# Parameter chains on GpSimd, rotation products summed in PSUM, second half's statistics between the first half's scalings

## What is computed

```python
u = group_norm(x)                                   # 16 x 96 x 256
fx = _layernorm(u, ln1_g, ln1_b)
step = jnp.exp(log_step)
lam_bar = jnp.exp(lam * step)                       # 48 complex modes
B_bar = ((lam_bar - 1.0) / lam)[:, None] * Bc
Bu = jnp.einsum('ph,blh->blp', B_bar, fx)
# xs[l] = lam_bar * xs[l-1] + Bu[l]
y = 2.0 * jnp.real(jnp.einsum('hp,blp->blh', Cc, xs)) + D * fx
y = jax.nn.gelu(y, approximate=False) + fx
fy = _layernorm(y, ln2_g, ln2_b)
z1, z2 = jnp.split(fy @ W_enc.T, 2, axis=-1)
out = x + (z1 * jax.nn.gelu(z2, approximate=False)) @ W_dec.T + fy
```

## Time and profile before

| | us |
|---|---|
| median of 3 runs | 112.12 (110.3 to 112.47) |
| profiled execution | 110.42 |
| its span | 108.6 |
| TensorE matmul busy | 94.9 (87%) |
| VectorE busy | 77.6 (71%) |
| ScalarE busy | 41.0 (38%) |
| GpSimd busy | 31.9 (29%) |
| granted TensorE clock, mean | 0.961 |

### The profile page before, as it was taken

The page is one execution under the profiler, slowest core; times in us unless marked ns, Lnnn a source line. Parts: engine busy times, 40 slices in busy tenths (PEclk is TensorE's granted clock), DMA queues, the critical chain, the costliest instruction groups (busy, mean ns, idle before and its releaser), DMA issues.

```text
span 108.6 us, 1488 instructions
## 1 busy us (share of the span) xinstructions
PE 94.9 (87%) x502; PEld 56.2 (52%) x502; DVE 77.6 (71%) x260; ACT 41.0 (38%) x79; POOL 31.9 (29%) x26
## 2 busy tenths in 40 slices
PE   5999897269989929999899999999599999999960
PEld 4668766146555715676476655567324432533310
DVE  1688999999986899658677302389990289994590
ACT  2254167807449100024037009818049722024200
POOL 8600000400049992000018000007995000296000
PEclk9999999955799999999999999999999999999997
DMA  2997000000000000000000000000000000450135
GB/s 77 275 262 168 3 0 0 6 0 0 0 0 0 0 0 3 0 6 0 0 0 0 0 0 3 6 0 0 0 0 0 0 0 0 118 149 29 28 84 177
DMA packets 3767, 3.79 MB, mean 35 GB/s; under 512 B 496, under 2 KB 3664, under 8 KB 3760
## 3 DMA queue, kind: packets, MB, share of 16 engines
q1 hardware_dynamic: 3392, 3.49, 12.3%
q10 hardware_dynamic: 368, 0.20, 0.8%
HBM read 2.12 MB, written 1.57 MB: 34 GB/s over the span
## 4 chain that ended last, share of the span: by engine, by line
PE 70%; DVE 21%; issue 4%; ACT 1%; DVEq 1%
PE ps L424 70%; DVE st L836 2%; DVE fy L664 2%; DVE pm L885 2%; DVE sc L694 2%; DVE rs L664 1%; DVE upper L668 1%; DVE sq L664 1%; DVE tb L664 1%; DVE tb L668 1%; DVE y L982 1%; DVE gn L664 1%; DVE rs L694 1%; DVE fx L664 1%; DVE sc L664 1%
## 5 line engine op out<-in xcount | busy, mean ns | idle before, releaser
L424 PE MATMUL ps<-fy,mt 96*96 96x512 f32 x32 | 14.9, 600 | 1.3 <-DVE fy L664 1.3
L290 POOL TENSOR_TENSOR y<-gl,fx 96x512 f32<-96x512 f32 x4 | 6.1, 1524 | 29.8 <-ACT gl L379 29.8
L298 POOL TENSOR_TENSOR res<-fy,xs 96x512 f32<-96x512 f32 x8 | 10.7, 1359 | 11.6 <-DVE fy L664 11.5
L424 PE MATMUL ps<-xs,pm 96*96 96x256 f32 x32 | 10.8, 492 | 3.3 <-DVE pm L885 3.3
L385 ACT ACTIVATE y<-ps,vecs 96x512 f32<-96x512 f32 x8 | 5.5, 687 | 16.4 <-PE ps L424 16.4
L664 DVE SCALAR_TENSOR_TENSOR w<-ps,vecs,y 96x512 f32<-96x512 f32 x8 | 5.9, 743 | 7.4 <-ACT y L385 7.4
L424 PE MATMUL ps<-fx,dm 96*96 96x512 f32 x16 | 8.4, 605 | 2.6 <-issue 2.2
L933 DVE TENSOR_TENSOR Z<-Z,ps 96x240 f32<-96x240 f32 (+3 forms) x8 | 2.8, 355 | 9.5 <-PE ps L424 9.5
L424 PEld LDWEIGHTS ps<-fy,mt 96*96 96x96 f32 x32 | 5.0, 163 | 8.7 <-issue 6.8
L424 PEld LDWEIGHTS ps<-xs,pm 96*96 96x96 f32 x32 | 6.4, 214 | 5.9 <-DVE pm L885 3.8
L379 ACT ACTIVATE gl<-ps,db 96x512 f32<-96x512 f32 x8 | 5.5, 684 | 9.4 <-PE ps L424 9.4
(11 more groups left out here) (112 smaller groups left out, 168.1 us busy)
## 6 DMA issues: line engine op xcount, KB each, us to landing
out_dram<-sq SPq DMA_DIRECT2D x8, 192.0 KB, 2.2
xs<-x_dram SPq DMA_DIRECT2D x3, 384.0 KB, 6.1
xs<-x_dram SPq DMA_DIRECT2D x2, 192.0 KB, 3.5
mt<-mats_dram SPq DMA_DIRECT2D x1, 338.6 KB, 6.8
mt<-mats_dram ACTq DMA_DIRECT2D x1, 180.0 KB, 3.9
sm<-small_dram ACTq DMA_DIRECT2D x1, 8.6 KB, 2.8
cmask<-mask_dram ACTq DMA_DIRECT2D x1, 9.0 KB, 4.9
```

The source lines that it names most:

```text
L290: nc.gpsimd.tensor_tensor(yv[:, RT * i:RT * (i + 1), :], cols(gl, H, i).rearrange("c (b m) -> c b m", b=RT), cols(fx, H, i).rearrange("c ( ...
L298: nc.gpsimd.tensor_tensor(cols(res, H, i), cols(fy, H, i), xs[:, HB * H + 2 * i:HB * H + 2 * i + 2, :].rearrange("c n l -> c (n l)"), ALU. ...
L424: return nc.tensor.matmul(o, lhsT, rhs, start=start, stop=stop)
```

## The change

[...] VectorE keeps seven column instructions at the start (`mode_columns`), the reciprocal of the exponential (`exp_inverse`, after the sixth statistics), and the bias column of `bst` (`input_bias`, after the first inverse sigma). GpSimd writes the sine matrices `rotS` and the cosine matrices `rotC` apart, and TensorE sums the two products with `bst` in PSUM. GpSimd makes `yl` before `rotX`. The second half's statistics 3 to 7 stand between the first five scalings of the first half, statistics 1 and 2 within the first group norm. Fourteen warm-up matmuls are added ahead of the second half's centering. `gelu_y` also waits for `db_ready`. The two generators and `parameter_steps` are gone.

```diff
...
-WARM = (10, 2, 14)
+WARM = (10, 2, 14, 14)
 WARM_N = 256
-FIRST_PM = 4
...
+            def expm1_column(p, y, arg):
+
+                settle()
+                ts(y, arg, 1 / 128, -80 / 128, ALU.mult, ALU.max)
+                settle()
+                ts(p, y, 1 / 120, None, ALU.mult)
+                for c in (1 / 24, 1 / 6, 1 / 2, 1.0):
+                    settle()
+                    ts(p, p, c, y, ALU.add, ALU.mult)
+                for _ in range(7):
+                    settle()
+                    ts(p, p, 2.0, p, ALU.add, ALU.mult)
+
+            def expm1_table(p, y, q, arg):
+
+                settle()
+                ts(y, arg, 1 / 128, -80 / 128, ALU.mult, ALU.max)
+                settle()
+                ts(p, y, 1 / 120, None, ALU.mult)
+                for c in (1 / 24, 1 / 6, 1 / 2, 1.0):
+                    settle()
+                    ts(q, p, c, None, ALU.add)
+                    settle()
+                    tt(p, q, y, ALU.mult)
+                for _ in range(7):
+                    settle()
+                    ts(q, p, 2.0, None, ALU.add)
+                    settle()
+                    tt(p, q, p, ALU.mult)
+
+            pool.wait_ge(in_small, 16)
+            pool.wait_ge(mode_ready, 4)
+            expm1_column(scol(EXP), scol(Y1), scol(REC))
+            settle()
+            nc.gpsimd.tensor_scalar(scol(EXP1), scol(EXP), 1.0, None, ALU.add).then_inc(exp_ready, 1)
+            pool.wait_ge(exp_inverted, 1)
+            tt(scol(T4), scol(REC1), scol(NEG), ALU.mult)
+            settle()
+            ts(scol(STEP), scol(EXP1), scol(POS), scol(T4), ALU.mult, ALU.add)
+            settle()
+            tt(scol(TH), s(LI), scol(STEP), ALU.mult)
+            tt(scol(RE), s(LR), scol(STEP), ALU.mult)
+            settle()
+            ts(tbl(ANG), s(KV, NK), scol(TH), None, ALU.mult)
+            ts(tbl(XK), s(KV, NK), scol(RE), None, ALU.mult)
+            settle()
+            ts(tbl(NRND), tbl(ANG), 1 / (2 * np.pi), ROUND, ALU.mult, ALU.add)
...
+            for part in (TWO_PI_HI, TWO_PI_MID, TWO_PI_LO):
+                settle()
+                ts(tbl(RED), tbl(NRND), -float(part), None, ALU.mult)
+                settle()
+                tt(tbl(ANG), tbl(RED), tbl(ANG), ALU.add)
+            settle()
+            nc.gpsimd.tensor_scalar(tbl(RED), tbl(ANG), PI_BELOW, -PI_BELOW, ALU.min,
+                                    ALU.max).then_inc(angles_ready, 1)
+            expm1_table(tbl(EXM), tbl(TMP), tbl(RK), tbl(XK))
+
+            pool.wait_ge(sines_ready, 2)
+            tt(tbl(SH2), tbl(SH), tbl(SH), ALU.mult)
+            ts(tbl(NSS), tbl(SIN), s(RHO), None, ALU.mult)
+            settle()
+            ts(tbl(CM1), tbl(SH2), -2.0, None, ALU.mult)
+            ts(tbl(RK), tbl(EXM), 1.0, None, ALU.add)
+            settle()
+            ts(tbl(COS), tbl(CM1), 1.0, None, ALU.add)
+            pool.wait_ge(in_mats, 16)
...
             nc.gpsimd.tensor_tensor(
-                rotT[:, :, :], m(M_ID).unsqueeze(1).broadcast_to([96, T, 96]),
-                tbl(COS, T).unsqueeze(2).broadcast_to([96, T, 96]), ALU.mult).then_inc(rotcos_ready, 1)
-            pool.wait_ge(in_mats, 16)
+                rotS[:, :, :], m(M_SW).unsqueeze(1).broadcast_to([96, T, 96]),
+                tbl(NSS, T).unsqueeze(2).broadcast_to([96, T, 96]), ALU.mult).then_inc(rot_ready, 1)
+            settle()
+            nc.gpsimd.tensor_tensor(
+                rotC[:, :, :], m(M_ID).unsqueeze(1).broadcast_to([96, T, 96]),
+                tbl(COS, T).unsqueeze(2).broadcast_to([96, T, 96]), ALU.mult).then_inc(rot_ready, 1)
+
+            tt(tbl(RSIN), tbl(RK), tbl(SIN), ALU.mult)
+            tt(scol(T1), tbl(EXM, 1, 1), tbl(COS, 1, 1), ALU.mult)
+            settle()
+            tt(scol(T3), tbl(RSIN, 1, 1), s(LI), ALU.mult)
+            tt(scol(T1), scol(T1), tbl(CM1, 1, 1), ALU.add)
+            settle()
+            tt(scol(T4), scol(T1), s(LI), ALU.mult)
+            ts(scol(CRE), scol(T1), s(LR), scol(T3), ALU.mult, ALU.add)
+            settle()
+            ts(scol(CIM), tbl(RSIN, 1, 1), s(LR), scol(T4), ALU.mult, ALU.subtract)
+            tt(scol(CRE), scol(CRE), scol(DEN), ALU.mult)
+            settle()
+            ts(scol(CIM), scol(CIM), scol(DEN), s(RHO), ALU.mult, ALU.mult)
+            settle()
+            ts(bt1[:, :], m(M_BS), scol(CIM), None, ALU.mult)
+            ts(bst[:, 0:C], m(M_B), scol(CRE), None, ALU.mult)
+            settle()
+            nc.gpsimd.tensor_tensor(bst[:, 0:C], bst[:, 0:C], bt1[:, :], ALU.add).then_inc(bst_ready, 1)
...
+            ts(tbl(SSG), tbl(SIN), s(NRHO), None, ALU.mult)
+            settle()
+            tt(tbl(RSSG), tbl(RK), tbl(SSG), ALU.mult)
+            settle()
+            tt(scol(ABSI), scol(ABSI), scol(STEP), ALU.mult)
+            settle()
+            ts(scol(MASK), scol(ABSI), float(np.float32(2 * np.pi)) / 4, 2.0, ALU.is_lt, ALU.mult)
+            settle()
+            tt(scol(MR), scol(MASK), s(NRHO), ALU.mult)
+            ts(scol(MI), scol(MASK), -1.0, None, ALU.mult)
+            settle()
+            ts(tbl(CU), tbl(COS), scol(MR), None, ALU.mult)
+            ts(tbl(SU), tbl(SIN), scol(MI), None, ALU.mult)
+            for dst, unit in ((XCO, COS), (XSI, SSG)):
+                ts(tbl(dst, 1, 0), tbl(unit, 1, T), tbl(RK, 1, 1), tbl(RK, 1, 0), ALU.mult, ALU.mult)
+                ts(tbl(dst, 1, 1), tbl(unit, 1, K16), tbl(RK, 1, 1), tbl(RK, 1, T), ALU.mult, ALU.mult)
+                tt(tbl(dst, 4, 2), tbl(unit, 4, K16), tbl(RK, 4, K16), ALU.mult)
+            nc.gpsimd.tensor_tensor(db[:, :], s(DD), s(B1), ALU.mult).then_inc(db_ready, 1)
+            nc.gpsimd.tensor_scalar(dm[:, :], m(M_ID), s(DD), None, ALU.mult).then_inc(dm_ready, 1)
+            settle()
...
-            pool.wait_ge(tables_ready, 1)
+            combine(yl, M_C, tbl(CU, T), M_CS, tbl(SU, T), T).then_inc(yl_ready, 1)
             combine(rotX, M_ID, tbl(XCO, NX), M_SW, tbl(XSI, NX), NX).then_inc(rotx_ready, 1)
-            combine(yl, M_C, tbl(CU, T), M_CS, tbl(SU, T), T).then_inc(yl_ready, 1)
             pool.wait_ge(yl_ready, 1)
             nc.gpsimd.tensor_tensor(yl[:, 1], yl[:, 0], tbl(RK, T).unsqueeze(2).broadcast_to([96, T, 96]),
                                     ALU.mult).then_inc(yl_ready, 1)
...
+            warm_up(WARM[3], bank(1, 0))
             center_batch(1, 0)
             group_bias(1)
...
             pe.wait_ge(taken[0], HB)
             pe.wait_ge(bst_ready, 1)
-            pe.wait_ge(rot_ready, T)
-            mm(bank(0, 2)[0:97, 0:480], bst[:, :], rotT[:, 0:5, :])
-            mm(bank(0, 3)[0:97, 0:288], bst[:, :], rotT[:, 5:8, :]).then_inc(umat_done, 1)
+            pe.wait_ge(bias_col_ready, 1)
+            pe.wait_ge(rot_ready, 2)
+            for part, first, last in ((2, 0, 5), (3, 5, 8)):
+                o = bank(0, part)[0:97, 0:96 * (last - first)]
+                mm(o, bst[:, :], rotS[:, first:last, :], stop=False)
+                last_mm = mm(o, bst[:, :], rotC[:, first:last, :], start=False)
+            last_mm.then_inc(umat_done, 1)
...
+            def mode_columns():
+
+                dve.wait_ge(in_small, 16)
+                stt(scol(REC), s(LS), -1.0, s(LS), ALU.mult, ALU.max).then_inc(mode_ready, 1)
+                norm.add(nc.vector.tensor_tensor(scol(T2), s(LR), s(LR), ALU.mult))
+                scaled(scol(NEG), s(LS), 0.0, None, ALU.is_lt).then_inc(mode_ready, 1)
+                scaled(scol(POS), s(LS), 0.0, None, ALU.is_ge).then_inc(mode_ready, 1)
+                norm.next_stt(scol(DEN), s(LI), s(LI), scol(T2), ALU.mult, ALU.add)
+                stt(scol(ABSI), s(LI), -1.0, s(LI), ALU.mult, ALU.max).then_inc(mode_ready, 1)
+                norm.settle()
+                nc.vector.reciprocal(scol(DEN), scol(DEN)).then_inc(den_ready, 1)
+
+            def exp_inverse():
+
+                dve.wait_ge(exp_ready, 1)
+                nc.vector.reciprocal(scol(REC1), scol(EXP1)).then_inc(exp_inverted, 1)
+
+            def input_bias():
+
+                dve.wait_ge(bst_ready, 1)
+                norm.add(nc.vector.tensor_tensor(bt1[:, :], bst[:, 0:C], m(M_B1), ALU.mult))
+                norm.settle()
+                nc.vector.reduce_sum(bst[:, C:C + 1], bt1[:, :],
+                                     axis=mybir.AxisListType.X).then_inc(bias_col_ready, 1)
+
...
-            dve.wait_ge(in_small, 16)
-            parameter_steps(6)
+            mode_columns()
             for q in range(HB):
                 statistics(0, q)
-                parameter_steps(1)
+                if q == HB - 3:
+                    exp_inverse()
             dve.wait_ge(in_early, 16)
             statistics(1, 0)
-            group_norm(0, lambda: parameter_steps(1), lambda: (statistics(1, 1), parameter_steps(2)))
+            group_norm(0, lambda j: None, lambda: (statistics(1, 1), statistics(1, 2)))
             for n in range(HB):
                 scale_centering(0, n)
-                if n % 2:
```

(37 more changed lines are left out.)

141 lines of the change are left out of this document (16 added, 125 removed).

## The result

| | before | after |
|---|---|---|
| median, us | 111.45 (110.3 to 112.47, 4 runs) | 114.34 (113.59 to 114.56, 4 runs) |
| profiled execution, us | 110.42 | 114.56 |
| its span, us | 108.6 | 112.7 |
| start of the second broadcast (the marker), us | 46.09 | 49.98 |

The ratio is 1.0332, with a 95% interval of 1.024 to 1.0423: the change made the kernel slower. The span grew by 4.1 us and the marker moved by 3.9, so nearly everything happened before the marker.

What follows compares the result with a forecast made beforehand. VectorE bounds the first part, TensorE or something it waits for the rest. Product start 29.5 us at half clock moves the marker from 46.09 to 47.5: 111.8 us profiled, 113.5 carried to the median, 112.8 taken; range 107 to 117.

Steps and rivals of the forecast that it cites:

- the point: Whole kernel: the middle case's 112.8 us, taken between 111.8 on the profiled time and 113.5 carried to the median.
- the second rival: GpSimd chain: dependent steps longer than 0.335 us; at 0.40 us the marker is 6.4 us late, 116.8 us; chance 0.38.
- signs of being wrong: Trace: GpSimd spacing 0.25 or less with product before 27 us, spacing 0.4, or TensorE waiting longer for inverse sigma than bias column.
- The count of 59 steps: GpSimd chain up to bias_col_ready: 59 dependent steps counted from the diff, each behind a settle.
- the gain of the front: Before the input matrix product: start near 25 instead of 29.93 us, almost 5 us, less 1.3 us for the doubled product.
- S: GpSimd chain: length of one dependent step, taken as 0.30 us, 0.32 in effect with collisions.
- the prediction's formula: GpSimd chain up to the input matrix product: U = 10.65 + 59 S = 29.5 us.
- U: Start of the input matrix product as set by GpSimd's chain: 29.5 us, against 29.93 before.
- the collisions: Small VectorE and GpSimd steps blocking each other over SBUF: 1.2 us lost on GpSimd, about 1 us on VectorE.
- the clock should hold: TensorE, second half's centering: 14 added warm-ups fill 18.3 to 20.9 us, so eight batches take 0.49 us each.
- the forecast mechanism: Input matrix product: TensorE idles 3.2 us until GpSimd's chain releases the bias column, then runs at half clock, 5.2 us.
- the hole: TensorE's 2.21 us of idle time before 40.05 us, waiting for GpSimd's yl; claimed gone with yl before rotX.

Runs made afterwards that it cites:

- the first experiment: Changed kernel with VectorE's reciprocal of the column exponential moved inside the first group norm; ratio 1.0344 to the kernel before, median 114.68 us.
- the product-sums experiment: Kernel before with only the input matrix product changed: rotC and rotS written apart, two products summed by TensorE; ratio 1.0, median 111.05 us.
- the last experiment: Changed kernel with rotS and rotC built behind bst instead of ahead of its factors; ratio 1.0189 to the kernel before, median 114.91 us.
- the split chain: Changed kernel with column exponential, step, angles and cosines back on VectorE, rotS and rotC behind bst, bias column inside first inverse sigma; ratio 0.9722, median 109.34 us.

## Why the prediction was right or wrong

**The number is right by its width.** The measured 114.34 us lies inside 107 to 117, and 1.5 us above the point of 112.8. But 1.0 us of that point is no mechanism: it was added to carry the sum from the profiled execution to a median. On the profiled execution the forecast is 111.8 and the result 114.56, +1.4 us against +4.1. The point said "within 2%"; slower by over 2% had a chance of 0.37 and belonged to the second rival. And one of the prediction's own signs of being wrong came true: what held the product longest was VectorE's inverse sigma (to 32.98 us), behind which the bias column stands, and not GpSimd's `bst` (31.12 us).

**Right: the place.** The marker carries the whole change: span +4.1, marker +3.9. The count of 59 steps stands. That the gain of the front hangs on GpSimd's chain holds as soon as VectorE is on time.

**Right in kind, too small: the chain.** By the prediction's own sum `bst` should be ready at 29.05 us; it was at 31.12. Term by term, from the trace after:

- Column exponential, 14 steps: 4.80 us (4.53 to 9.33) for 4.48. A step whose second operand is a column scalar takes 0.35 (3.85 us for 11).
- Reciprocal there and back: 0.28 for 0.3.
- Angles, 13 steps and their side instructions: 4.64 us (9.61 to 14.25), as counted (some 4.6).
- Table exponential, 24 steps: 7.6 us, 0.317 each, for 7.7.
- From `SH2` to `COS`: 1.3 for some 1.3. `rotS` and `rotC`: 2.9 for 3.0.
- Five steps of the factors: 2.7 us (26.13 to 28.83) for some 2.05. Three of their instructions have two column scalars and take 0.33 to 0.44 each without the wait.
- Three 96x96 instructions: 2.3 us (28.83 to 31.12) for 1.2. The two tensor_scalar ones, 1.08 and 0.76, ran beside VectorE's scalings and inverse sigma; with the reciprocal moved and VectorE idle they took 0.54, 0.51 and 0.38, 1.5 us in all, still more than forecast from the products over 576 and 768 elements.

So S for table steps was right at 0.32, and the excess of 2.1 us is column scalars (1.0) and the 96x96 instructions (1.1). A slip in the prediction does not touch this sum: eight batches of 0.49 us from 20.9 us on end at 24.8, not 24.5, which makes the expected idle time 2.9 and not 3.2 us. Put in the prediction's formula, the product of the first experiment at 32.15 us would be S = 0.364 in effect: the side of its second rival, long steps, which decides from 30.4 us. That rival gave +6.4 us at U = 34.3; at 32.15 that is about 4.2, and the first experiment's marker moved by 4.1.

**Right by half: the collisions.** The forecast let small steps collide with small steps, 1.2 us on GpSimd and 1 us on VectorE. This hardly happened: GpSimd's table steps took 0.317, and first group norm steps beside them 0.20 each, for the 0.19 of an unmixed step. What does collide is a small VectorE step with a large GpSimd instruction. The rule cited from the Trainium skill (SBUF — State Buffer, Who interferes with whom) makes one instruction block while the other runs, and the 1.2 to 1.5 us of the stalls agree (`rotC` alone is 1.47); the prediction used it for the wrong pair. As the prediction tells it, for VectorE instructions with two SBUF inputs, it does not cover all of them: the earlier trace rows already had a step with one input among the three (L669, 1.24 us). The prediction had two large instructions, `rotS` and `rotC`, in its sum and did not ask what VectorE does then. In the kernel after that is the second group norm, 2.4 us, in the product-sums experiment two steps.

**Wrong: where the clock falls.** The prediction had the exponential make the first mean end 0.8 us late, at 10.05 us (it ended 1.4 late: 10.32 + 0.31 against 9.25), and carried only the delay. The wait also opened a gap of 1.20 us on TensorE, and from about 11.5 to 21.7 us it ran at 1.2 GHz; the gap filled, it did not. The mean of the second half was forecast at 15.75 us; it was at 17.28 with the gap filled and at 21.60 without. I had written that the clock should hold and looked only at idle time ahead of the second centering, as in the earlier trace rows.

**Wrong: who releases the product.** The forecast said GpSimd's chain. In the kernel after VectorE came last: 5.9 us from the late mean and 2.4 us from the stalls, which more than cover the 7.7 by which inverse sigma was late (32.98 us instead of 25.3), behind `bst` at 31.12. TensorE had idled 1.18 us, the clock was whole, and the product took 2.8 us, not 5.2. With either fault of the front removed, the forecast mechanism appears, with a longer idle time than the 3.2 us forecast: 5.3 or 6.4 us idle, VectorE's bias column released by GpSimd, product at half clock, marker at 50.0 to 50.2. Two bounds lie within 2 us of each other, and the product at half clock (2.6 us longer) more than closes that distance. In the first experiment the forecast 29.5 us of the product became 32.15: 2.3 us of chain and 0.4 between `bst` and the product; its marker went from the forecast 47.5 to 50.16. So in that kernel the size of the miss is the chain's. In the kernel after it is the balance of two errors: the product started 4.2 us later than forecast (33.68 for 29.5) and, at full clock, took 2.4 us less (2.8 for 5.2), and the stalls saved 0.7 us less; together 2.5 us, the marker's 49.98 for 47.5. Nothing in the traces ties these two errors to the chain's 2.7 us; that they come out alike looks like chance.

**Right: behind the product.** With `yl` before `rotX` the hole is gone, as forecast. The saving in stalls was 0.5 us for 1.2 forecast, as the scans were later by 5.0 us while GpSimd was later too (`yl` at 40.8 for 37.3).

**Not settled.** Why the clock of the kernel after is back at 22 us and that of the last experiment at about 17.5, with the same first mean at 10.32 us, no run explains. What the nearly 3 us of stalls in the second inverse sigma would be worth with smaller `yl` and `rotX` instructions was not tried.

## What to carry to other kernels

A long chain of dependent small operations pays its price by the step, not by the element: about 0.31 us on GpSimd (0.35 with a column scalar) where VectorE's is 0.19, so move the branches that nobody waits for, and leave the one that the next stage waits for where steps are short, as the split chain did (0.972, and 1% or more against the best of the kernel before). When an engine's late part is repaired, ask at once which other input of the same wait is next: here three repairs of the front moved the marker by 0.3 us at most. Where a wait is added, look at TensorE's gap as well as at the delay, and place large GpSimd instructions where VectorE has nothing small on the path.
